# From tile 14 on, DMA instead of TensorE turns the activation codes of a fused attention and FP4 MLP kernel

## The reference

```python
# x: (8, 1024, 256); 16 heads of 16 features
q, k = elu(x @ Wq + bq) + 1, elu(x @ Wk + bk) + 1
k = k / sqrt(sum(k * k, per head) + 1e-6);  v = x @ Wv + bv
attn = (q @ k.T) @ v                        # per head, no softmax
y = layernorm(x + attn @ Wo + bo, eps=1e-6) * gamma + beta
x1 = layernorm(x + y, eps=1e-5)

def fp4_quant_dequant(x):                   # blocks of 16 along the last dimension
    scale = maximum(max(abs(xb)) / 6, 1e-12)
    return GRID[searchsorted(MID, abs(xb / scale))] * sign(xb) * scale
def fp4_linear(x, w):
    return fp4_quant_dequant(x) @ fp4_quant_dequant(w).T

h = silu(fp4_linear(x1, w_gate)) * fp4_linear(x1, w_up)     # 704 features
out = layernorm(x1 + fp4_linear(h, w_down), eps=1e-5)
```

## Time and profile before

| | |
|---|---|
| median of 3 runs | 700.19 us (700.13 to 703.07) |
| profiled execution, its own time | 700.59 us |
| span of the profiled execution | 698.9 us |
| granted TensorE clock, mean | 0.998 |
| busy share of PE, DVE, ACT, POOL | 98%, 84%, 70%, 87% |
| chain that ended last | PE 91% |

### The profile page before, as it was taken

How to read it: one execution, slowest core, us unless ns; L and a number is a source line. 1 busy time by engine, 2 the same in 40 slices (tenths; PEclk the granted TensorE clock), 3 DMA queues, 4 the chain that set the end, 5 groups by cost and what they waited for, 6 DMA issues and landing times.

```text
span 698.9 us, 14240 instructions
## 1 busy us (share of the span) xinstructions
PE 683.4 (98%) x4370; PEld 602.8 (86%) x4370; DVE 584.1 (84%) x1441; ACT 489.3 (70%) x954; POOL 608.8 (87%) x947
## 2 busy tenths in 40 slices
PE   8999999999989999999999999999999999999995
PEld 6888888888868799999999999999999999999995
DVE  6678678876778899889989998998998998998774
ACT  4677777766777676777677677677767767767664
POOL 3988898988888998899989989899899988989766
PEclk9999999999999999999999999999999999999999
DMA  8544443344301111122211122122111211100001
GB/s 267 189 136 136 136 140 117 131 157 155 107 32 34 58 47 46 45 78 75 76 66 57 36 86 80 57 76 76 46 61 62 77 45 47 61 17 16 21 28 45
DMA packets 23135, 56.36 MB, mean 81 GB/s; under 512 B 2642, under 2 KB 5908, under 8 KB 23060
## 3 DMA queue, kind: packets, MB, share of 16 engines
q1 hardware_dynamic: 22640, 55.32, 23.4%
q10 hardware_dynamic: 420, 0.13, 0.1%
HBM read 30.22 MB, written 25.17 MB: 79 GB/s over the span
## 4 chain that ended last, share of the span: by engine, by line
PE 91%; DVE 2%; POOL 2%; issue 2%; ACT 1%; DMA 1%; SPq 0%; POOLq 0%; DVEq 0%
PE banks L407 23%; PE banks L408 22%; PE banks L409 22%; PE banks L553 8%; PE banks L524 7%; PE banks L445 2%; PE banks L418 2%; PE banks L567 1%; PE banks L566 1%; PE banks L431 1%; PE banks L476 1%; DMA arena<-in_L_attn_x_dram 1%; PE banks L484 1%; POOL arena L1164 1%; DVE actT_lo L958 0%
## 5 line engine op out<-in xcount | busy, mean ns | idle before, releaser
L407 PE MATMUL banks<-wgu_hi,actT_lo 128*128 128x512 f32 (+1 forms) x384 | 149.8, 390 | 1.6 <-DVE actT_lo L958 1.4
L408 PE MATMUL banks<-wgu_lo,actT_hi 128*128 128x512 f32 (+1 forms) x384 | 144.0, 375 | 0.0
L409 PE MATMUL banks<-wgu_hi,actT_hi 128*128 128x512 f32 (+1 forms) x384 | 143.3, 373 | 0.0
L725 ACT ACTIVATE arena<-banks 128x512 f32<-128x512 f32 x64 | 38.4, 600 | 111.8 <-PE banks L409 111.6
L1164 POOL TENSOR_TENSOR arena<-arena 128x960 f32<-128x960 f16 (+2 forms) x68 | 115.3, 1695 | 0.0
L1140 POOL TENSOR_TENSOR arena<-arena 128x704 f32<-128x704 f32 x64 | 91.8, 1434 | 20.5 <-DVE arena L945 18.6
L407 PE MATMUL banks<-wd_hi,actT_lo 128*128 128x256 f32 x320 | 100.1, 313 | 0.0
L958 DVE TENSOR_TENSOR actT_lo<-banks,actT_hi 128x512 fp32r<-128x512 f32 (+1 forms) x132 | 85.5, 674 | 16.9 <-ACT actT_hi L711 16.2
L409 PE MATMUL banks<-wd_hi,actT_hi 128*128 128x256 f32 x320 | 90.2, 282 | 0.0
L408 PE MATMUL banks<-wd_lo,actT_hi 128*128 128x256 f32 x320 | 90.2, 282 | 0.0
L407 PEld LDWEIGHTS banks<-wgu_hi,actT_lo 128*128 128x128 f32 x384 | 72.5, 189 | 11.2 <-DVE actT_lo L958 2.3
(11 more groups left out here) (126 smaller groups left out, 1917.3 us busy)
## 6 DMA issues: line engine op xcount, KB each, us to landing
xs<-x_plus_scratch SPq DMA_DIRECT2D x32, 512.0 KB, 3.3
x_plus_scratch<-xs SPq DMA_DIRECT2D x24, 512.0 KB, 2.9
arena<-in_L_attn_x_dram SPq DMA_DIRECT2D x32, 256.0 KB, 3.5
out_dram<-arena SPq DMA_DIRECT2D x32, 256.0 KB, 2.1
x_plus_scratch<-arena SPq DMA_DIRECT2D x4, 512.0 KB, 2.9
x_plus_scratch<-resid SPq DMA_DIRECT2D x4, 512.0 KB, 2.6
resid<-in_L_attn_x_dram SPq DMA_DIRECT2D x4, 256.0 KB, 3.9
resid<-in_L_ffn_w_down_dram SPq DMA_DIRECT2D x1, 704.0 KB, 8.0
```

The costliest lines, as they stand in the source:

```text
L407: nc.tensor.matmul(dst, sl, mh, start=(k == 0), stop=False, skip_group_check=shared)
L408: nc.tensor.matmul(dst, sh, ml, start=False, stop=False, skip_group_check=shared)
L409: last = nc.tensor.matmul(dst, sh, mh, start=False, stop=(ended and k == n - 1), skip_group_check=shared)
```

## The change

For tiles n >= 14 (`by_dma`) PE no longer transposes `va`.

- SP, step n-2: `turn_codes(n)` issues one DMA transpose of the two-byte codes, `vqc` (128 x 1024) to `codes` (in the space of `wo_sb`, one buffer). It waits for `cut(n)` and for the dequantisation of tile n-1.
- PE, step n-3: `scales_turn(n)` transposes the 60 columns of `s14` into PSUM; ACT `scales_copy(n)` copies them to `sT`.
- SP, step n-3: `spread_scales(n)` writes `sT` to memory (three DMAs), waits for them, and reads each row back 16 times, once for each feature of a block, into `s_each` (512 KB, two buffers in the space of `resid` tiles 0 to 7).
- POOL, step n-2: `dequantise_turned(n)` is one instruction over 1024 columns with a full tensor of scales as second input, in place of two instructions of 64 and 960 columns in which a scale is repeated for 16 columns.
- ACT, start of step n-1: `high_turned(n)`, from SBUF, in 896 and 128 columns. DVE: `low_turned(n)`, one instruction over 1024 columns whose two inputs are both in SBUF, in place of two of 512 columns that read PSUM and SBUF.
- ACT rounds the 64 repeated columns as well (one more small instruction), `cut` goes over 16 rows of 64 instead of 15.
- PE does `attend(t+9)` ahead of `gate_up(t, 2)`, and the late loads and adds for x (`X_AGAIN`) are moved to steps 21, 27, 33, 39 from 14, 22, 30, 38.

```diff
+        BY_DMA = 14
+        codes = wo_sb[:, :, :].rearrange("p k d -> p (k d)").bitcast(U16).rearrange("p (c n) -> p c n", c=VC)
...
-        X_AGAIN = {14 + 8 * i: DEFER + i for i in range(NP - DEFER)}
+        X_AGAIN = {21 + 6 * i: DEFER + i for i in range(NP - DEFER)}
...
+                if by_dma(t + 2):
+                    turn_codes(t + 2)
+                if by_dma(t + 3):
+                    spread_scales(t + 3)
+
+            def turn_codes(n):
+                sp.wait_ge(round_s, n + 1)
+                sp.wait_ge(deq_s, n)
+                sp.dma_start_transpose(codes, vqc[n % 2].bitcast(U16)).then_inc(codes_in, 16)
+
+            def spread_scales(n):
+                i = n - BY_DMA
+                sp.wait_ge(sT_s, i + 1)
+                after(sp, s_each_in[n % 2], 16 * (i // 2))
+                whole = (VC - 1) * GC
+                sp.dma_start(s_turned[n % 2, :, 0:VC - 1, :].rearrange("g c t -> c g t"),
+                             sT[0:whole, :]).then_inc(sT_out, 16)
+
+                half = GC // 2
+                for k in range(2):
+                    sp.dma_start(s_turned[n % 2, k * half:(k + 1) * half, VC - 1, :],
+                                 sT[whole:whole + half, :]).then_inc(sT_out, 16)
+                sp.wait_ge(sT_out, 3 * 16 * (i + 1))
+                if i < 2:
+                    sp.wait_ge(r3_s, 4 * i + 4)
+                sp.wait_ge(deq_s, n - 1)
+                sp.dma_start(s_each[n % 2].rearrange("p c n -> p (c n)"),
+                             s_turned[n % 2].rearrange("g c t -> g (c t)").unsqueeze(1).broadcast_to(
+                                 [GC, BLK, VC * P])).then_inc(s_each_in[n % 2], 16)
...
+            def scales_turn(n):
+                pe.wait_ge(scale_s, n + 1)
+                after(pe, sT_s, n - BY_DMA)
+                nc.tensor.transpose(ps[0:VB, T_BANK, 0:P], s14[:, n % 2, :], ident[:, :]).then_inc(sT_ps, 1)
...
-                if joint(t + 1):
+                if by_dma(t + 3):
+                    scales_turn(t + 3)
+                if joint(t + 1) and not by_dma(t + 1):
                     turn(t + 1)
+                if by_dma(t + 1) and there(t + 9):
+                    attend(t + 9)
                 if there(t):
                     gate_up(t, 2)
-                if there(t + 9):
+                if not by_dma(t + 1) and there(t + 9):
                     attend(t + 9)
...
+            def high_turned(n):
+                act.wait_ge(deq_s, n + 1)
+                if there(n - 2):
+                    act.wait_ge(gu_ps, 3 * n - 3)
+                act.wait_ge(dn_ps, n - 1 - LAG)
+                a, v = chunks(n)[0], v_turned(n)
+                nc.scalar.activation(vT_hi[:, n % 2, a:VC - 1, :], v[:, a:VC - 1, :], ACT.Copy).then_inc(vT_hi_s, 1)
+                nc.scalar.activation(vT_hi[:, n % 2, VC - 1, :], v[:, VC - 1, :], ACT.Copy,
+                                     scale=upper[:, :]).then_inc(vT_hi_s, 1)
...
             def step(t):
+                if by_dma(t + 1):
+                    high_turned(t + 1)
                 if there(t):
                     silu(t, 0)
...
+                if by_dma(n):
+                    b = VC * P
                 nc.vector.tensor_scalar(lines(vqc[n % 2].bitcast(U16)[:, a:b]), vqb[n % 2][:, a // RW:b // RW, 0:RW],
                                         ROUND_MASK, None, ALU.bitwise_and).then_inc(round_s, 1)
...
+            def low_turned(n):
+                a, v = chunks(n)[0], v_turned(n)
+                dve.wait_ge(vT_hi_s, 2 * n + 2)
+                nc.vector.tensor_tensor(vT_lo[:, n % 2, a:VC, :], v[:, a:VC, :], f32(vT_hi[:, n % 2, a:VC, :]),
+                                        ALU.subtract).then_inc(vT_lo_s, 1)
...
+            def dequantise_turned(n):
+                a = chunks(n)[0]
+                pool.wait_ge(codes_in, 16 * (n - BY_DMA + 1))
+                pool.wait_ge(s_each_in[n % 2], 16 * ((n - BY_DMA) // 2 + 1))
+                pool.wait_ge(vT_lo_s, n - 1)
+                nc.gpsimd.tensor_tensor(v_turned(n)[:, a:VC, :], codes[:, a:VC, :].bitcast(F16), s_each[n % 2][:, a:VC, :],
+                                        ALU.mult).then_inc(deq_s, 1)
```

More of the change, by code:

```diff
@@ L54, in build @@
     x_plus = nc.dram_tensor("x_plus_scratch", (NP, P, 4 * D), F32, kind="Internal").ap()
+    GC = P // BLK
+    s_turned = nc.dram_tensor("scales_scratch", (2, GC, VC, P), F32, kind="Internal").ap()
     with ExitStack() as ctx:
@@ L208, in build @@
         vT_ps, vT_hi_s, vT_lo_s = sem("vT_ps"), sem("vT_hi"), sem("vT_lo")
+        sT_ps, sT_s, sT_out, codes_in = (sem(n) for n in ("scales_turned", "scales_copied", "scales_out", "codes_in"))
+        s_each_in = [sem(f"scales_in{i}") for i in range(2)]
         gu_ps, g_act, h_s = sem("gu_ps"), sem("g_act"), sem("h_done")
@@ L260, in joint, with by_dma @@
             return there(n) or there(n - LAG)
+        def by_dma(n):
+            return joint(n) and n >= BY_DMA
         def columns(n):
@@ L551, in turn @@
                 after(pe, vT_lo_s, n)
+                after(pe, sT_s, n + 3 - BY_DMA)
                 for c in range(c0, c1):
@@ L696, in to_f16 @@
                 after(act, round_s, n - 1)
+                if by_dma(n):
+                    nc.scalar.activation(vqb[n % 2][:, RN, 0:RW].bitcast(F16), halves(vy[:, n % 2, VW - RW:VW]), ACT.Copy,
+                                         scale=F16_ONE)
                 nc.scalar.activation(vqb[n % 2][:, a // RW:b // RW, 0:RW].bitcast(F16), lines(halves(vy[:, n % 2, a:b])),
@@ L757, in step @@
                     ln3_apply(t - 6, t)
-                if joint(t + 1):
+                if by_dma(t + 3):
+                    scales_copy(t + 3)
+                if joint(t + 1) and not by_dma(t + 1):
                     high(t + 1)
```

28 lines of the change are left out of this document (21 added, 7 removed).

## The result

The changed kernel takes 833.06 us (median of 4 runs, 829.42 to 836.16) against 701.31 for the kernel before in the same comparison (4 runs, 700.13 to 703.07): 1.187 times as long, interval 1.182 to 1.193. The forecast was 749 us, in a range of 712 to 845. The direction and the range held; the loss is 132 us where 49 were forecast.

What follows compares the result with a forecast made beforehand. PE was taken to set the pace, 7.58 us a step, with POOL near; POOL's step would become 8.2. Steady part 27 us, last ten steps 18 and eight steps 4 give 49 more: 749 us, range 712 to 845.

Steps and rivals of the forecast that it cites:

- Relief of PE: Transposes taken off PE: its step becomes 6.9 us, worth 0.69 us a step if nothing else stood at that height.
- Dequantisation on POOL: POOL's one 1024-column multiplication takes 2.34 us instead of 2.00, bounds 1.9 and 2.4; POOL's work becomes 7.27 us.
- Exclusion: DVE's remainder with two SBUF inputs blocks POOL: 0.9 us a step, bounds 0 and 1.15; POOL's step 8.2 us.
- below 9 us: If the second to issue blocks fully: POOL loses 1.15 us, pace 8.4, total below 9 us higher.
- Cut: DVE's cut over 16 rows instead of 15: 0.4 us taken, bounds 0.36 and 0.36 + 1.4.
- The ring: Dequantisation, scales and sum, cut, DMA transpose, hand-overs wait in a circle: pace not below 4.2 us plus the transpose's landing.
- L: DMA transpose from issue to landing: 3.9 us taken, between 2.1 and 3.9 by the nearest rows; pace 8.1 us.
- The scales' trip: Scales through PE, ACT, memory and read-back: 8 to 9 us altogether, hidden by some 12 us of lead.
- Rival (b): The transpose itself is slow, over 4.4 us, and its ring sets the pace: 803 or 858 us; chance 0.36.
- Rival (d): Faster: POOL's dequantisation takes no longer than before, pace about 6.95 us, 673 us; chance 0.12 for 673 to 696.
- Rival (c): DVE blocking POOL costs little, as POOL waits for the transpose anyway: pace 7.3 to 7.8, 700 to 730 us; chance 0.12.
- The last ten steps: End of the kernel, where PE has less to do: 79 us against 61.2, 18 us more.

Runs made afterwards that it cites:

- e11: Changed kernel without the scales' trip from tile 16, block scales not waiting for the multiplication, remainder reading PSUM: 701.63 us, ratio 1.000.
- e1: Changed kernel without the scales' way through memory from tile 16 on, old scales used: 749.25 us, ratio 1.069.
- e10: Changed kernel without the scales' trip from tile 16, and block scales on DVE no longer waiting for the multiplication: 740.96 us, ratio 1.056.
- e4: Changed kernel with DVE's remainder taking its first input from an idle PSUM bank instead of SBUF: 830.93 us, ratio 1.186.
- e12: Changed kernel with block scales not waiting for the multiplication, read-back from 16 rows, and issued on ACT's queue: 775.04 us, ratio 1.105.
- e3: Changed kernel with the DMA transpose replaced by a plain copy of the same 256 KB, codes not turned: 820.14 us, ratio 1.170.
- e7: Changed kernel with the read-back of the scales issued by ACT at the end of its step instead of by SP: 795.04 us, ratio 1.135.

## Why the prediction was right and wrong

**Relief of PE: about right in size, and worth nothing.** PE has idle time before its matmuls and 30% of the chain. In e11, at a granted clock of 1.00, it is busy 92.5 of 100 us, some 7.0 us of a mean step of 7.54 (forecast 6.9). There an undisturbed step gained 0.42 us of the 0.69, and then POOL's step is the limit.

**Dequantisation on POOL: right.** 2.15 us, between the bounds of 1.9 and 2.4, 0.2 under the value taken.

**Exclusion: right in size, hidden here.** 0.86 us for 0.9. It sets the pace only where the DMA does not (7.98 us in e1, 8.15 in e10, forecast 8.2); in the changed kernel it lies inside the wait (e4). By the page SBUF — State Buffer of the Trainium skill, the second to issue blocks fully until the first is done. The trace agrees: POOL comes 0.38 us later and loses the rest of DVE's instruction. The 1.15 us that I had priced for that rule is the case in which both start together, and "below 9 us" was too little even for that: 43 x (8.42 - 8.17) is 11 us.

**Cut: right in 34 of 43 steps.** It takes 0.42 us for 0.4, but 1.2 to 1.5 where it meets POOL's L1230, within my bounds, and more where it runs beside the multiplication (1.61 us in e12, 1.91 in e11, above my bound of 1.76).

**The ring: right in form.** The pace is a fixed part plus L. With all hand-overs the fixed part is 4.15 us in the mean for the 4.2 taken, but that is partly luck: it is 3.8 in a plain step, and the steps with the add for x, which I had at 0.5 us more, cost 1.6 to 2.4 us more, since the add pushes the cut into the exclusion.

**The failed step: "I take 3.9, the dearest of its size, since it moves in two-byte pieces: pace 8.1, just under POOL's".** L was 5.8 us in the median and 5.9 in the mean. It is the mis-sized term, and it turned the path round: the pace is 10.03 us and the ring's, not 8.2 and POOL's. 43 x (10.03 - 8.2) is 79 of the 86 us by which the profile's 135 exceed the forecast of 49. It was mis-sized because of another sentence: "The scales' trip: ... 8 to 9 us altogether ... hidden". Hidden it was, as a latency: the read-back landed at least 0.9 us before its use in every step. I costed the trip as a latency to be covered, with the read-back at 3.3 us, and the queue at its old DMA share of 0.21. But a transfer that nobody waits for still occupies the engines and the queue that the awaited one needs. The read-back adds 512 KB to each step, at 7.0 us in the median, and the share rises to 0.65. Alone (e1) the transpose takes 3.1 us, inside my bounds of 2.1 to 3.9 and below what I took.

**Rival (b)** gave the form of the sum and nearly the numbers (L = 5: 803 us, L = 6: 858) but not the reason. "Single two-byte elements change partition" is refuted by e3, where a plain copy lands about as late. Of the two pages weighed there, Advanced Engine Details and Errata (such DMAs as fast as regular ones) agrees with e3, except for the issue on SP. VectorE: DVE Perf Modes, by which I estimated 10.5 us for eight blocks in a row, does not agree with the 3.1 us of e1.

**Rival (d)**, faster, was to decide at 2.66 us for multiplication and exclusion together; they are 2.15 + 0.86 = 3.01, so it was rightly refused, though e11 shows that without the exclusion (2.15) it would not have come either. **Rival (c)**, L of 3 to 3.6 with the exclusion inside a wait, does not occur: with L at 3.1 (e1) POOL's step is the limit.

**The last ten steps** took 84.5 us for the 79 forecast, 66.8 in e1. **The loss by cause**, from the medians: the scales' trip 84 us (changed kernel to e1), exclusion and ring together 48 (e1 to e11), the rest under 1 (e11 to the kernel before). In that rest the relief of PE and the late transposes cancel.

## What to carry to other kernels

When work moves from an engine to DMA, add up the busy time of the DMA engines per step, helper transfers included, before calling any of them hidden: a covered transfer still delays the one on the path. Look at the order too: a store issued 0.7 us behind the bulk transfer landed in 6.3 us, one issued ahead of it in 2.3, while a change of queue alone showed next to nothing. (To issue the transpose itself ahead of the read-back was not tried.) Give a transfer an outermost dimension of 16 rather than 8 where that is possible (45 us here), and do not replicate data by way of memory if an engine can repeat it as it reads: half the replicated bytes gave back 78 us. Where two limits lie within half a microsecond of each other, test the removal of both together: neither price is seen alone.

## What the runs showed that I had not expected

- A read-back of 8 rows, each repeated 16 times, takes 7.0 us in the median for 512 KB and lands in 8 parts, where a plain load of that size takes 3.3; from 16 rows, each repeated 8 times, it lands in 16 parts and takes 4.7.
- A DMA transpose of 128 x 1024 two-byte codes from SBUF to SBUF lands in 3.1 us when little else is under way, and holds SP for 1.23 to 1.27 us at most of its issues (up to 2.8 in the changed kernel), a plain copy for 0.53.
- A transpose issued some 3 us behind the read-back never landed before it, whether the two were in one queue (changed kernel) or in two (e7); the nearest came 0.8 us behind in both.
- The steps with one more DVE add in the ring cost 1.6 to 2.4 us more and not 0.5, since the cut behind it comes to lie beside a POOL instruction and takes 1.2 to 1.4 us instead of 0.42.
- The granted clock fell from 0.998 in the mean to 0.925, and to 0.84 between 400 and 500 us, a mixture of the two levels of 2.4 and 1.2 GHz, where PE stood idle for several us within a step. In e10, with steady steps of 8.1 us, it was 1.00 in that window at almost the same busy share of PE (84% and 81%). What the lower clock costs was not measured apart; no instruction of PE is part of the ring, and it held up the cut in one of the 43 steps, by 0.3 us.
